# Thirty-two small register loads on TensorE become eight larger ones, the first couple of them ahead of the stage that uses them

## The reference, cut to what matters

```python
x  = L0(x)                                   # attention, experts of layer 0
xn = layernorm(x)
s  = gated_linear_attention(xn)              # a recurrence over the tokens, then an MLP
logits   = xn @ router_w                     # 64 experts
topk_idx = top_k(logits + router_bias, 4)    # four experts for a token
comb     = normalised softmax scores at topk_idx, 0 elsewhere
g = silu(einsum('nd,edf->nef', xn, wg));  u = einsum('nd,edf->nef', xn, wu)
routed = einsum('ne,nef,efd->nd', comb, g * u, wd)
shared = a gated MLP that every token goes through
x = x + s * silu(routed + shared)
```

## Time and profile before

| | |
|---|---|
| runs of the kernel, three | 1194.11, 1194.45, 1199.62 us; median 1194.45 us |
| the profiled execution's own time | 1192.11 us |
| its span in the trace | 1190.4 us |
| busy share of the span | PE 88%, DVE 71%, ACT 53%, POOL 49% |
| mean granted TensorE clock | 0.944 of full speed |

### The profile page before, as it was taken

The page is one execution under the profiler, slowest core; times in us unless marked ns, Lnnn a source line. Parts: engine busy times, 40 slices in busy tenths (PEclk is TensorE's granted clock), DMA queues, the critical chain, the costliest instruction groups (busy, mean ns, idle before and its releaser), DMA issues. The chain is left out here.

```text
span 1190.4 us, 23472 instructions
## 1 busy us (share of the span) xinstructions
PE 1045.4 (88%) x7870; PEld 697.7 (59%) x7870; DVE 842.4 (71%) x1461; ACT 628.1 (53%) x1241; POOL 586.6 (49%) x449
## 2 busy tenths in 40 slices
PE   6776878999999999789999999999978967878797
PEld 4355666666666666556666666657833335457444
DVE  3958427687878787667778778884579955856557
ACT  3536137666666666556666666662351024645531
POOL 3540325586657665745776575543228302531164
PEclk9875799999999999989999999999999978989899
DMA  5136120976786666538657755565102316658832
GB/s 169 40 102 179 28 53 1 108 79 76 82 103 73 94 64 105 78 48 100 75 92 68 100 77 84 48 87 146 46 30 80 111 62 206 205 187 274 284 92 89
DMA packets 186058, 119.82 MB, mean 101 GB/s; under 512 B 64548, under 2 KB 179286, under 8 KB 185686
## 3 DMA queue, kind: packets, MB, share of 16 engines
q1 hardware_dynamic: 170070, 97.35, 46.2%
q10 hardware_dynamic: 12800, 12.58, 3.0%
q0 software_dynamic: 3072, 8.39, 2.1%
HBM read 81.90 MB, written 36.37 MB: 99 GB/s over the span
## 5 line engine op out<-in xcount | busy, mean ns | idle before, releaser
L1297 DVE TENSOR_REDUCE a_nmax<-psum 128x1 f32<-128x1024 f32 x128 | 156.1, 1219 | 80.0 <-PE psum L1145 76.1
L1303 DVE SCALAR_TENSOR_TENSOR a_pT<-psum,a_pT 128x512 f16<-128x512 f32 x256 | 164.9, 684 | 22.3 <-ACT a_pT L1240 16.7
L1240 ACT ACTIVATE a_pT<-psum 128x512 f16<-128x512 f32 x256 | 140.4, 604 | 18.1 <-PE psum L1156 11.7
L1058 POOL TENSOR_TENSOR a_rnorm<-a_ss,a_power 128x8 f32<-128x8 f32 x32 | 58.3, 1823 | 181.6 <-DVE a_ss L1273 181.6
L1232 ACT ACTIVATE a_ex<-psum,a_nmax 128x1024 f32<-128x1024 f32 x128 | 142.8, 1116 | 9.4 <-issue 8.6
L1156 PEld LDWEIGHTS psum<-ident,a_ex 128*128 128x128 f32 x1024 | 119.5, 141 | 25.8 <-DVE a_pT L1303 1.4
L1156 PE MATMUL psum<-ident,a_ex 128*128 128x128 f32 x1024 | 133.3, 273 | 0.0
L1127 PE MATMUL psum<-a_wh,xT_h 128*128 128x128 f16 (+1 forms) x512 | 115.6, 248 | 2.0 <-PEq L2738 2.0
L1129 PE MATMUL psum<-a_wh,xT_l 128*128 128x128 f16 (+1 forms) x512 | 115.4, 248 | 0.3 <-issue 0.3
L1128 PE MATMUL psum<-a_wl,xT_h 128*128 128x128 f16 (+1 forms) x512 | 115.5, 248 | 0.0
L1167 PE MATMUL psum<-a_pT,a_vh 128*128 128x512 f16 x256 | 97.5, 381 | 14.8 <-DVE a_of L976 13.7
(11 more groups left out here) (394 smaller groups left out, 2584.0 us busy)
## 6 DMA issues: line engine op xcount, KB each, us to landing
split_gate_up<-a_e_wh SPq DMA_DIRECT2D x64, 128.0 KB
a_rb<-row_scales SPq DMA_DIRECT2D x32, 256.0 KB, 4.2
g_e_gu<-split_gate_up SPq DMA_DIRECT2D x32, 256.0 KB, 3.8
block_outputs<-g_e_ym ACTq DMA_DIRECT2D x16, 512.0 KB, 4.4
split_rest<-a_e_wh SPq DMA_DIRECT2D x45, 128.0 KB
wf<-in_L_ffn_W_gate SPq DMA_DIRECT2D x32, 128.0 KB, 2.5
wf<-in_L_ffn_W_up SPq DMA_DIRECT2D x32, 128.0 KB, 2.5
wf<-in_L_ffn_W_down SPq DMA_DIRECT2D x32, 128.0 KB, 3.0
```

Source lines behind the costliest of these rows:

```text
L1240: act.activation(pT[g][:, 0, 4 * h:4 * h + 4, (m % 4) * P:(m % 4 + 1) * P], bank_of(r, unit).rearrange("p (k q) -> p k q", k=4), ACT.Copy, ...
L1297: dve.tensor_reduce(nmax[:, k:k + 1], score_banks(m), AX.X, ALU.max, negate=True).then_inc(max_ready, 1)
L1303: dve.scalar_tensor_tensor(low, bank_of(r, unit).rearrange("p (k q) -> p k q", k=4), PROB, high, ALU.mult, ALU.subtract).then_inc(low_done, 1)
```

## The change

The rows are read in four groups of twelve pairs in place of sixteen groups of three. A group is two loads: one of 16 registers for its eight main pairs, one of 8 registers for its four extra pairs. The first group is read at step 12 of the recurrence, between spread_values(14) and gathered_step(12), with the wait for the table that it needs there. The other three are read at q = 4, 16 and 28, at the place in the loop where they stood before, ahead of down(q).

```diff
-    WEIGHTS, HIDDEN = 8, 3
+    WEIGHTS, HIDDEN, GROUP = 8, 3, 4
@@
-    def rows_at(self, pe, i):
-        main, extra = 2 * self.order[3 * i], 2 * self.order[3 * i + 2]
-        for first, many, pairs in ((main, 4, (3 * i, 3 * i + 1)), (extra, 2, (3 * i + 2,))):
+    def rows_at(self, pe, g):
+        main, extra = ([q for q in range(3 * self.GROUP * g, 3 * self.GROUP * (g + 1)) if (q % 3 == 2) == last]
+                       for last in (False, True))
+        for pairs in (main, extra):
+            first = 2 * self.order[pairs[0]]
             _, places = self.nc.values_load_multi_w_load_instructions(
-                self.table[0:1, first:first + many], engines=[pe.engine], min_val=0, max_val=SLOTS1,
+                self.table[0:1, first:first + 2 * len(pairs)], engines=[pe.engine], min_val=0, max_val=SLOTS1,
...
@@ the recurrence, on PE
                 if s == 2:
                     pe.wait_ge(router.table_ready, 3)
                     values(1, 6)
+                if s == STEPS - 4:
+                    pe.wait_ge(router.table_loaded, 16)
+                    blocks.rows_at(pe, 0)
@@ the pairs, on PE
             wait_sorted(pe)
-            blocks.rows_at(pe, 0)
...
-                if q % 3 == 0 and q + 3 < PAIRS:
-                    blocks.rows_at(pe, q // 3 + 1)
+                if q % (3 * blocks.GROUP) == 4 and q + 3 * blocks.GROUP < PAIRS:
+                    blocks.rows_at(pe, q // (3 * blocks.GROUP) + 1)
                 blocks.down(pe, q)
```

## The result

The changed kernel takes 1189.32 us (median of 8 runs, 1186.16 to 1190.99) against 1194.7 us of the kernel before (median of 8, 1190.03 to 1199.62), ratio 0.9947, 95% interval 0.9924 to 0.9970. The forecast was 12.4 us less, 1182.0; the medians differ by 5.4 us, and by the interval the kernel is 3.6 to 9.1 us faster. The direction holds, and the time lies in the range (1177.5 to 1190.5). The size doesn't hold: less than half came. The profiled executions lie nearer to each other than the medians: they took 1192.11 us before and 1190.99 after, with spans of 1190.4 and 1189.2 us.

The account below looks back on a forecast made before the run. PE was taken as nearest its limit in the pairs stage, stalled by register loads no semaphore shows. Saved 14.9 - 4.2 for new groups + 1.7 for the clock = 12.4 us, from 1194.45 to 1182.0 us; range 1177.5 to 1190.5.

Parts of the forecast that it names:

- The loads in the loop: Ahead of down(q): fifteen couples of loads leave, gaps of 15.1 us, of which 13.8 us were counted as saved.
- The first couple in the recurrence: Moving the loads from ahead of gate_up(0) into PE's 1.87 us wait saves 1.1 us at price 0.
- The new groups: Three groups of loads at q = 4, 16 and 28 cost 1.4 us each, 4.2 us together.
- The slope of 23 ns a register: Register loads on PE: each further register adds about 23 ns, so a group takes 1.3 us in quiet.
- The traffic's 0.8 us on top: Register loads in the busy pairs stage: 0.8 us more than in quiet, making 2.1 us a group.
- The price for each register: Rival, chance 0.11: load time goes with registers, three groups cost 10.5 us, 4.4 us less, 1190.0 us.
- the dear end: Groups at q = 4, 16, 28: 155 ns a register, 3.7 us a group, gaps of 10.5 us for three.
- The slower rival: Rival, chance 0.04: each register pays the traffic delay, 6.9 us a group, 3.7 us more, 1198 us.
- What stays covered: Pairs stage: weights, ordered eight pairs ahead, stay in time though PE gets some 12 us earlier.
- The clock: After the stalls at q = 36 and 42: one of two low-clock stretches saved, 1.7 us, range 0 to 3.4.
- The base: Whole kernel: the profiled execution of 1192.11 us gave the terms; the runs' median, 1194.45 us, was the reference.

Follow-up runs that it names:

- e3: Kernel before, with only the first two register loads (4 and 2 registers) moved to step 12 of the recurrence; ratio 0.9970.
- e9: Kernel before, with the MLP's weight pieces loaded from q = 36, not 32, and W2 behind the last pair's weights; ratio 1.0016.
- e2: Kernel before, with the first piece of the MLP's weights loaded at q = 36 in place of q = 32; ratio 0.9993.
- e5: The changed kernel unedited, measured again on another chip against the kernel before; ratio 0.9931.
- e11: Changed kernel with the two loads of each group swapped, 8 registers first, then 16; one run, 1187.82 us, no ratio.
- e1: Changed kernel, with the first piece of the MLP's weights loaded at q = 36 in place of q = 32; ratio to before 0.9920.
- e7: Changed kernel, with W2, the last third of the MLP's weights, loaded behind the last pair's weights; ratio to before 0.9914.
- e10: Changed kernel, with the MLP's weight pieces loaded from q = 36 and W2 behind the last pair's weights; ratio to before 0.9926.
- e6: Changed kernel, MLP pieces from q = 36, groups moved ahead of down(6), between down(15) and side(15), ahead of down(33); ratio to before 0.9869.
- e4: Changed kernel, with four old couples of 4 and 2 registers at q = 33, 36, 39, 42 replacing the group at q = 28; ratio to before 0.9951.

## Why the prediction was wrong

**The loads in the loop.** Right in kind; the size is less certain than it looks. At down(36) the steps give 1.1 us for the first couple and 10.9 us for the nine gaps up to there, less 4.2 for the new groups: 7.8 us. The two profiled executions show 8.2. But from the first gate_up to down(36) the four kernels with the old loads in the loop took 114.5 (before), 117.4 (e3), 117.9 (e9) and 120.8 us (e2). The six with the new groups at q = 4, 16 and 28 (change, e5, e11, e1, e7, e10) took 107.3 to 109.2. Some of both kinds have the MLP's weights moved. The means, 117.6 and 108.0, differ by 9.6 us where the steps give 6.7. So the close agreement rests on the shortest of four traces, and the loads were probably worth more than I said, not less.

**The first couple in the recurrence.** Right. gathered_step(12) still waits 1.87 us for DVE, as in the earlier trace rows, and the gap before the first gate_up is 1.03 us.

```profile
953.30 3.16 PE L2024 MATMUL psum<-g_qs,g_gather_h 128*128 128x512 f32 x4 [1.87 <-DVE g_qs L2246]
```

**The new groups.** Their sum is right, 1.36 + 1.65 + 0.92 = 3.9 us against 4.2, but by two errors that cancel. The slope of 23 ns a register, between SP's load and PE's, was too small; it is 64. The traffic's 0.8 us on top was too large: a group takes 1.75 to 2.13 us. The price for each register is thus real but under half of the dear end's 155 ns. The trace of this case also lies far below the 200 ns of the Trainium skill ("Runtime: NRT & Kernel Launch", "Instruction fetch mechanics"), which by the prediction's estimate would have made 4.8 us of a group. The slower rival wanted 6.9 us of a group in traffic; the one at q = 4, with a DMA share of 0.88, took 2.1, so it falls too.

**"What stays covered" is the step that failed.** It said that weights are ordered eight pairs ahead and have 11 us or more. I took the buffers' rule, q waits for down(q - 8), for SP's own time, and looked neither at what else stands on SP's queue nor at the last third of the stage, where SP was already 2 to 8 us behind the freed buffers (pair 33's first load was issued at 1083.55, and down(25), which frees its buffer, ended at 1076.5). At pair 44 only 3.8 us lay between the last issue and the use, and the change was to make PE 12 us earlier. This rival, a transfer that becomes late when PE gets faster, wasn't on my list. It took back 5.6 us of the 8.2 between down(36) and the MLP, where the steps had a further 2.95 us of gain. The loss repeats: this last part took 22.7 to 23.7 us in the four kernels with the old loads, 28.9 to 30.0 in the three traces of the change (change, e5, e11), and 23.9 in e10, which differs from the change only in when SP loads the MLP's weights.

**The clock.** I took 1.7 us as saved after the stalls at q = 36 and 42. In their place the waits for weights stand, and the clock is low behind them: 0.50 from 1102 to 1106, after PE had stood idle for 3.92 us, and 0.91 over the stage against 0.93. The term was sized by stalls that I took to vanish, and other stalls came to the same place.

**The base.** The sum was made against one execution. The stage of the kernel before and of the kernels with its loads took 138.2, 143.5, 140.6 and 140.7 us, so the profiled one was at the short end. How far single traces differ shows in e2. Its edit only takes effect once SP has loaded pair 32, which waits for down(24), and its down(24) already comes 3.8 us later behind the first gate_up than in the kernel before (85.7 against 81.9). The profiled execution of the change, 1190.99 us, was the longest of its eight runs. That is why the two traces differ by 1.2 us and the medians by 5.4.

**Left open.** How exactly the late weights divide between SP's stand and the traffic. In the last part of the stage each easing alone leaves 26.1 or 26.2 us of some 29.4, and both together 23.9, so the two count about alike. Each of these is one trace, the ratios' intervals overlap, and the second easing adds nothing to e6 in the ratio. Why the register loads take so different a time from one execution to the next is open too: the gap at q = 36 is 1.38 to 2.67 us in the four kernels with the old loads. The last stage is 1.4 us longer in the change's trace (61.6 against 60.2 us), but that is no effect of the change: over all thirteen traces it takes 59.0 to 65.3 us, 61.2 in e5 and 64.4 in e9, which has the old loads.

## What to carry to other kernels

When an engine gets faster by more than a few microseconds, compare, for each transfer that it will need, the time of its issue with the time of its use, in the tightest part of the stage and not on average, and read the issuing queue's own waits: one wait for something unrelated holds back all that stands behind it. A register load is an invisible stall of the engine whose sequencer runs it; in e4 it cost nothing where the engine waited for weights anyway, so such a wait is where it belongs. Trust a saving of some microseconds only against more than one execution.

## What I had not expected of the hardware

- A register load grows by 64 ns a register, whatever its place in a couple: 333 ns for 4, 588 for 8, 1104 for 16. A load of 2 behind one of 4 takes 533 ns or more, above this line; I have no cause for it.
- The first load after a semaphore wait took 0.19 us more than its like: 519 ns (e3) against 333, 779 against 588, 1288 against 1104, all at step 12 with a DMA share of 0.00. That the wait is the reason is inferred; no run leaves it out.
- Issuing one DMA on SP took 2.78 us, where most take some 0.5 us. The DMA share was 0.94 meanwhile. A full DMA alone doesn't explain it: at 1112.19 and 1112.82, with a share of 1.13, two issues took 0.59 and 0.47 us.
